# VectorE reads the attention's numerator and denominator in PSUM, tile by tile

## The chip, the cores and the metric

One core of one Trainium2 chip runs the whole program. The metric is device time in microseconds, from launch to end of one execution; the median of several executions counts. TensorE (PE) multiplies matrices into PSUM, VectorE (DVE) and ScalarE (ACT) work on SBUF and PSUM, GpSimd (POOL) works on SBUF and starts the indirect transfers, SyncE (SP) starts the other transfers.

## What is computed

Two blocks follow each other on x, of shape (2, 512, 128), that is 1024 tokens of 128 values. Each block adds a cross-attention to a context of 77 tokens (16 heads of 8 values) and then a mixture of 8 experts, of which each token takes 2. Cut to the part that matters here, one attention is

```python
scores = jnp.einsum('bhqd,bhkd->bhqk', q, k) * SCALE     # block 0 adds a bias
attn = jax.nn.softmax(scores, axis=-1)
attended = jnp.einsum('bhqk,bhkd->bhqd', attn, v)
attended = attended.transpose(0, 2, 1, 3).reshape(B, L_q, D_MODEL)
attended = attended @ Wout.T + b_out                      # block 1: ctx @ W_O + b_O
gate = jax.nn.sigmoid(attended @ Wgate.T + b_gate)        # block 0 only
output = gate * attended + (1.0 - gate) * residual
```

The kernel takes the softmax's division behind the sum over keys: it forms a numerator (probabilities times values) and a denominator (probabilities times ones), both with one column per query and one row per head and value, and divides.

## The kernel before

The 1024 tokens are 8 tiles of 128, two tiles make a query group g (GQ = 256 queries), and there are 4 groups. A unit u is 4 of the 16 heads for one group, so there are 16 units in an attention and units 4g to 4g + 3 belong to group g. Attention a (0 and 1) runs over the units in turns. In turn u, TensorE does the shifted scores of unit u (L1178, in attention 0 with the bias, L1184), the transposed maxima of unit u + 1 (L1162), the scores of unit u + 2 (L1153) and `attend` of unit u - 2 (L1201: 4 matmuls into the numerator bank BNUM, 4 into the denominator bank BDEN, accumulated over the 4 units of the group). From turn 14 on there are no more scores to issue. VectorE reduces the scores of a unit to their maxima (L804), ACT takes the exponential (L654) and copies the maxima into the stack (L638).

The steps that follow on a finished group are laid into the turns by tables (`PE_STEPS`, `DVE_STEPS`, `ACT_STEPS`, `POOL_STEPS`): step `name` of group g comes in turn 4g + 3 + delay on its engine, behind the unit's own work, and in the order of the table where several fall in one turn. Names with a 3 are for the last group. Each engine works in program order; between engines there are only semaphores. The steps named here:

- `attended` (VectorE, L809 to L815): reciprocal of the denominator (L813), times the numerator (L814) into attT. It works on ACT's copy `numden` in SBUF, which ACT makes in `attention` (L643 to L649).
- `attend` (TensorE, L1188) of the first unit of the next group waits on `s_nd`, ACT's copy (L1197), since it overwrites the banks.
- `project` (TensorE, L1205 to L1219): attT times the output weights, in attention 0 also transposed (L1214), into bank BY. In attention 0, ACT then adds the bias to the transposed half (`projected`, L667), VectorE reads the other half (`projected`, L823), TensorE computes the `gate` (L1226, L1227) into the same bank, and ACT takes its tanh (L661). The next group's `project` waits for that tanh.
- `residual` (VectorE, L833 and L835, or L840 and L843) and the statistics, then GpSimd's `deviation` (L500, L501), then `hidden` (VectorE, L796, into hidk), `turn` (TensorE's transposes, L1138), `turned` (ACT, L679), `logits` (TensorE, L1243), `choose` (VectorE, L859 or L862 to L876), `ranks` (TensorE, L1253), `slots` (VectorE, L883 to L889), `send` (GpSimd, L518). The experts begin when all rows are sent.

In turns 3 to 9, GpSimd also subtracts the low halves of the expert weights (L531), 2.4 us each. Behind unit 15, TensorE does some warm-up matmuls between the steps of attention 1 (`WARM_TAIL`), none in attention 0.

## Time and profile before

| | |
|---|---|
| median of 3 runs | 325.83 us (324.19 to 326.91) |
| profiled execution, its span | 324.3 us |
| TensorE busy | 250.7 us (77%) |
| VectorE busy | 155.1 us (48%) |
| ScalarE busy | 118.2 us (36%) |
| GpSimd busy | 137.8 us (42%) |
| chain that ended last | PE 49%, issue 20%, DVE 13%, DMA 6%, POOL 5%, ACT 3% |

The profiled execution's span lies within the times of the runs. The page also cuts the span into 40 slices of 8.1 us, with the busy share of each engine and the granted clock of TensorE in tenths:

```profile
PE   2767999999975539999942989989987338999800
DVE  3878425363775364242211964276878303332205
PEclk9999999999975558999995799999999959999975
```

Attention 0 with its tail lies at about 29 to 120 us, the experts of block 0 behind it, attention 1 with its tail at about 193 to 262 us. TensorE is busy nearly all the time in the loop of units and less so in the tail behind it, where in attention 0 the granted clock is at half for some slices. Busy times of an engine are no critical path: a wait is read from the timeline, by its place.

### The profile page before, as it was taken

To read this page: it belongs to the slowest core of one execution; us is meant where nothing else is said; L and a number is where in the kernel's file an instruction comes from. 1 tells how busy PE (TensorE), PEld (TensorE's weight loads), DVE (VectorE), ACT (ScalarE), POOL (GpSimd) and SP (SyncE) were. 2 spreads that over 40 slices of the span, in tenths; PEclk is the share of its full clock that TensorE was granted. 3 is DMA by queue.
4 is the path that set the end of the run, shared out by engine and by line. 5 is a ranking of instruction groups with operands and counts; after the bars stand their busy time and mean duration, and the time that the engine had idled before them with its cause. 6 is when DMAs were issued, how large, how long until landed. Compare 5 with 4: busy or idle time off the path is not lost.

```text
span 324.3 us, 5466 instructions
## 1 busy us (share of the span) xinstructions
PE 250.7 (77%) x2044; PEld 197.2 (61%) x2044; DVE 155.1 (48%) x497; ACT 118.2 (36%) x206; POOL 137.8 (42%) x178
## 2 busy tenths in 40 slices
PE   2767999999975539999942989989987338999800
PEld 2645766667754427999941775545555328999800
DVE  3878425363775364242211964276878303332205
ACT  4033637755321023443500067965540204423200
POOL 5744602630156441355562400641267631456640
PEclk9999999999975558999995799999999959999975
DMA  7999970200011017000013920200010125001015
GB/s 241 269 224 377 219 161 2 65 3 2 0 36 34 33 33 197 16 20 26 23 36 127 361 116 0 66 1 2 0 37 33 33 82 141 15 31 36 26 29 181
DMA packets 26819, 27.02 MB, mean 83 GB/s; under 512 B 3193, under 2 KB 23844, under 8 KB 26534
## 3 DMA queue, kind: packets, MB, share of 16 engines
q1 hardware_dynamic: 23797, 21.58, 24.6%
q0 software_dynamic: 2560, 4.08, 3.9%
q10 hardware_dynamic: 432, 0.98, 0.9%
q8 instruction: 18, 0.29, 0.4%
q14 instruction: 12, 0.09, 0.1%
HBM read 16.76 MB, written 10.79 MB: 85 GB/s over the span
## 4 chain that ended last, share of the span: by engine, by line
PE 49%; issue 20%; DVE 13%; DMA 6%; POOL 5%; ACT 3%; another core or an unknown queue 1%; SPq 1%; POOLq 0%; DVEq 0%; ACTq 0%
PE ps L1201 8%; PE ps L1406 6%; PE ps L1178 6%; PE ps L1395 5%; PE ps L1162 4%; PE ps L1153 4%; PE ps L1133 3%; PE ps L1184 2%; DMA xres<-x 2%; DMA xe<-back 2%; DVE cst L813 2%; DMA sent<-hidk,slotu 1%; DVE attT L814 1%; PE ps L1217 1%
## 5 line engine op out<-in xcount | busy, mean ns | idle before, releaser
L559 POOL DMA_INDIRECT back<-probT,pairu x48 | 46.5, 970 | 37.4 <-DVE probT L992 15.1
L1133 PE MATMUL ps<-blank,ident 128*128 128x256 f32 x90 | 28.6, 479 | 23.6 <-DMA sent<-hidk,slotu 13.0
L1406 PE MATMUL ps<-w,hT 128*128 128x128 f32 (+1 forms) x384 | 45.0, 274 | 0.0
L804 DVE TENSOR_REDUCE peak<-ps 128x8 f32<-128x616 f32 x32 | 25.5, 798 | 40.2 <-PE ps L1153 40.2
L1406 PEld LDWEIGHTS ps<-w,hT 128*128 128x128 f32 (+1 forms) x384 | 44.2, 183 | 0.0
L654 ACT ACTIVATE probT<-ps 77x1024 f32<-77x1024 f32 x32 | 32.7, 1022 | 27.7 <-PE ps L1184 15.5
L518 POOL DMA_INDIRECT sent<-hidk,slotu x32 | 31.9, 997 | 16.4 <-issue 9.8
L1133 PEld LDWEIGHTS ps<-blank,ident 128*128 128x128 f32 x90 | 21.1, 244 | 28.5 <-issue 14.0
L531 POOL TENSOR_TENSOR w1lo<-hT,w1hi 128x1024 fp32r<-128x1024 f32 x8 | 18.9, 2366 | 40.0 <-ACT w1hi L628 40.0
L1178 PE MATMUL ps<-qst,kst 100*78 100x256 f32 x128 | 29.1, 300 | 1.0 <-ACT qst L638 1.0
L500 POOL TENSOR_SCALAR vare<-mv 128x2 f32<-128x2 f32 (+2 forms) x17 | 3.8, 226 | 52.8 <-DVE mv L786 52.3
L696 ACT ACTIVATE hT<-ps,col 128x384 f32<-128x384 f32 x32 | 17.3, 582 | 24.1 <-PE ps L1395 24.1
L696 ACT ACTIVATE hT<-ps 128x321 f32<-128x321 f32 x32 | 13.3, 441 | 33.2 <-PE ps L1395 33.0
L1395 PE MATMUL ps<-xhi,w1hi 128*128 128x384 f32 (+1 forms) x64 | 22.2, 346 | 1.5 <-DVE xlo L981 1.5
L1178 PEld LDWEIGHTS ps<-qst,kst 100*78 100x78 f32 x128 | 16.9, 148 | 8.4 <-issue 5.8
L1162 PE MATMUL ps<-ident,peak 128*4 128x128 f32 x128 | 19.2, 273 | 2.9 <-DVE peak L804 2.9
L1201 PE MATMUL ps<-probT,vpad 77*32 77x256 f32 x256 | 21.0, 391 | 0.0
L1395 PE MATMUL ps<-xhi,w1lo 128*128 128x384 f32 (+1 forms) x64 | 20.8, 325 | 0.0
L1395 PE MATMUL ps<-xlo,w1hi 128*128 128x384 f32 (+1 forms) x64 | 20.8, 325 | 0.0
L1201 PE MATMUL ps<-probT,onepad 77*32 77x256 f32 x256 | 20.2, 379 | 0.0
L992 DVE TENSOR_TENSOR probT<-ps,row 128x128 f32<-128x128 f32 x24 | 5.5, 285 | 26.6 <-PE ps L1406 23.2
L995 DVE COPY probT<-ps 128x128 f32<-128x128 f32 (+1 forms) x24 | 5.5, 284 | 25.4 <-PE ps L1406 21.9
(158 smaller groups left out, 474.1 us busy)
## 6 DMA issues: line engine op xcount, KB each, us to landing
sent<-blank SPq DMA_DIRECT2D x16, 193.5 KB, 8.5
xe<-sent SPq DMA_DIRECT2D x16, 193.5 KB, 4.0
back<-blank SPq DMA_DIRECT2D x16, 128.0 KB, 4.8
hT<-w1b SPq DMA_DIRECT2D x4, 512.0 KB, 6.0
w<-w2b SPq DMA_DIRECT2D x1, 2048.0 KB, 13.5
xe<-back SPq DMA_DIRECT2D x8, 256.0 KB, 3.5
hT<-w1d SPq DMA_DIRECT2D x4, 512.0 KB, 5.5
w<-w2d SPq DMA_DIRECT2D x1, 2048.0 KB, 11.4
```

The source lines that it names most:

```text
L518: pool.indirect_dma_start(sent[m], bass.IndirectOffsetOnAxis(ap=slotu[:, t, k:k + 1], axis=0), hidk[:, t, k, :], None, bounds_check=NSLOT ...
L531: pool.tensor_tensor(w1lo[:, w, :], raw[:, k % RAWS], w1hi[:, w, :].bitcast(F32), ALU.subtract)\
L559: pool.indirect_dma_start(back[m], bass.IndirectOffsetOnAxis(ap=pairu[0:n, e, c:c + 1], axis=0), ye[0:n, e, c, :], None, bounds_check=NPAI ...
L654: act.activation(probT[0:KV, u % RING].rearrange("p (i q) t -> p i (q t)", i=2), ps[0:KV, BK:BK + 2, :], ACT.Exp).then_inc(s_exp[a], 1)
L696: act.activation(hT[:, e % 2, f, 0:CAP[m]], ps[:, 2 + n % 4, 0:CAP[m]], ACT.Silu, bias=bias).then_inc(s_silu[m], 1)
L804: dve.tensor_reduce(peak[:, u % 2], s, AX.X, ALU.max, negate=True).then_inc(s_peak[a], 1)
L1133: pe.matmul(ps[:, bank, 0:GQ], ident[:], blank[:, 0:2, 0:D], start=True, stop=True)
L1162: last = pe.matmul(ps[ST:ST + Q4, BK + u % 2, i * P:(i + 1) * P], peak[:, u % 2, i, :], ident[:], start=True, stop=True)
L1178: last = pe.matmul(ps[0:KP, BK + q // 2, GQ * (q % 2):GQ * (q % 2) + GQ], kst[0:ST + Q4, b, Q4 * j + q, :], qst[0:ST + Q4, j, at:at + GQ], ...
L1201: last = pe.matmul(ps[32 * q:32 * q + 32, bank, 0:GQ], w, probT[0:KV, u % RING, q, :], start=(j == 0), stop=(j == UG - 1))
L1395: last = pe.matmul(ps[:, 2 + n % 4, 0:EVEN[m]], w[:, e, f * P:(f + 1) * P], x[:, e % 2, 0:EVEN[m]], start=(i == 0), stop=(i == len(parts) ...
L1406: last = pe.matmul(ps[0:n, 6 + e % 2, c * P:(c + 1) * P], hT[:, e % 2, f, c * P:c * P + n], w2[:, e, f, :], start=(f == 0), stop=(f == FC ...
```

## The change

The `numden` copy, its semaphore `s_nd` and ACT's waits are gone. VectorE's `attended` comes one turn earlier (delay 4 in place of 5), waits for TensorE's last `attend` of the group (`s_pv`), and does reciprocal and multiply for one tile of 128 queries after the other, reading both from PSUM; each tile raises `s_att` by one, so a group raises it by GT = 2. `attend` of the next group's first unit and the key stack of attention 1 wait for all tiles by `s_att`. `project` waits for each tile and issues its matmuls per tile.

```diff
-DVE_STEPS = [dict(attended=5, projected3=6, residual3=7, hidden3=9, projected=8, residual=9, hidden=10,
+DVE_STEPS = [dict(attended=4, projected3=6, residual3=7, hidden3=9, projected=8, residual=9, hidden=10,
...
-             dict(attended=5, residual=7, hidden=8, choose=10, slots=11)]
+             dict(attended=4, residual=7, hidden=8, choose=10, slots=11)]
...
-        numden = cst[:, 0:2 * GQ].rearrange("p (i t) -> p i t", i=2)
...
-                g, rest = divmod(u - AHEAD - 1, UG)
-                if rest == UG - 1 and 0 <= g < GROUPS:
-
-                    act.wait_ge(s_pv[a], UG * (g + 1))
-                    if g >= 1:
-                        act.wait_ge(s_att[a], g)
-                    act.copy(numden, ps[:, BNUM:BDEN + 1, 0:GQ]).then_inc(s_nd[a], 1)
...
-                dve.wait_ge(s_nd[a], g + 1)
+                dve.wait_ge(s_pv[a], UG * (g + 1))
                 b, at = divmod(g, GROUPS // B)
-                link(dve.reciprocal(rden, numden[:, 1]))
-                dve.tensor_tensor(attT[:, b, GQ * at:GQ * at + GQ], numden[:, 0], rden, ALU.mult)\
-                   .then_inc(s_att[a], 1)
+                for i in range(GT):
+                    tile = slice(i * P, i * P + P)
+                    link(dve.reciprocal(rden[:, tile], ps[:, BDEN, tile]))
+                    q0 = GQ * at + i * P
+                    dve.tensor_tensor(attT[:, b, q0:q0 + P], ps[:, BNUM, tile], rden[:, tile], ALU.mult)\
+                       .then_inc(s_att[a], 1)
...
-                    pe.wait_ge(s_nd[a], u // UG)
+                    pe.wait_ge(s_att[a], GT * (u // UG))
...
-                pe.wait_ge(s_att[a], g + 1)
...
-                q0 = GQ * at
-                if a == 0:
-                    pe.matmul(ps[:, BY, 0:GQ], weight("out0"), attT[:, b, q0:q0 + GQ], start=True, stop=True)
                 for k in range(GT):
+                    pe.wait_ge(s_att[a], GT * g + k + 1)
+                    tile = attT[:, b, GQ * at + k * P:GQ * at + (k + 1) * P]
+                    if a == 0:
+                        pe.matmul(ps[:, BY, k * P:(k + 1) * P], weight("out0"), tile, start=True, stop=True)
                     o = (GQ if a == 0 else 0) + k * D
-                    last = pe.matmul(ps[:, BY, o:o + D], attT[:, b, q0 + k * P:q0 + (k + 1) * P],
-                                     weight("out0" if a == 0 else "o1"), start=True, stop=True)
+                    last = pe.matmul(ps[:, BY, o:o + D], tile, weight("out0" if a == 0 else "o1"), start=True, stop=True)
                 last.then_inc(s_yz, 1)
...
-                    pe.wait_ge(s_nd[0], GROUPS)
+                    pe.wait_ge(s_att[0], TILES)
```

On VectorE, in the loop of attention 0, the rows around `attended` of group 0 and group 1 stood so in the kernel before (L804 is the maxima reduction of a unit, L823 is `projected` of group 0, cst is the SBUF tensor that held the copy and the reciprocal):

```order
L804 TENSOR_REDUCE peak<-ps 128x8 [waits scores0] x5
L813 RECIPROCAL cst<-cst 128x256 [waits attended_in_sbuf0]
L814 TENSOR_TENSOR attT<-cst 128x256 [waits dve_order]
L804 TENSOR_REDUCE peak<-ps 128x8 [waits scores0] x3
L823 TENSOR_TENSOR hidb<-ps,hidb 128x256 [waits residual_ready,yT_in_sbuf,y_projected]
L804 TENSOR_REDUCE peak<-ps 128x8 [waits scores0]
L813 RECIPROCAL cst<-cst 128x256 [waits attended_in_sbuf0]
L814 TENSOR_TENSOR attT<-cst 128x256 [waits dve_order]
```

and stand so now:

```order
L795 TENSOR_REDUCE peak<-ps 128x8 [waits scores0] x4
L806 RECIPROCAL cst<-ps 128x128 [waits attended0]
L808 TENSOR_TENSOR attT<-ps,cst 128x128 [waits dve_order]
L806 RECIPROCAL cst<-ps 128x128
L808 TENSOR_TENSOR attT<-ps,cst 128x128 [waits dve_order]
L795 TENSOR_REDUCE peak<-ps 128x8 [waits scores0] x4
L806 RECIPROCAL cst<-ps 128x128 [waits attended0]
L808 TENSOR_TENSOR attT<-ps,cst 128x128 [waits dve_order]
L806 RECIPROCAL cst<-ps 128x128
L808 TENSOR_TENSOR attT<-ps,cst 128x128 [waits dve_order]
L817 TENSOR_TENSOR hidb<-ps,hidb 128x256 [waits residual_ready,yT_in_sbuf,y_projected]
```

The step has moved ahead of one reduction, and from group 1 on ahead of `projected` of the group before. On TensorE the same place of attention 0, attend of unit 4, had

```order
L1153 MATMUL ps<-kst,qst 128x312
L1201 MATMUL ps<-probT,vpad 32x256 [waits attended_in_sbuf0,probs0]
L1201 MATMUL ps<-probT,vpad 32x256 x3
L1201 MATMUL ps<-probT,onepad 32x256 x4
L1178 MATMUL ps<-qst,kst 78x256 [waits probs0,maxima_in_stack0]
```

and has now

```order
L1147 MATMUL ps<-kst,qst 128x312
L1195 MATMUL ps<-probT,vpad 32x256 [waits attT_ready0,probs0]
L1195 MATMUL ps<-probT,vpad 32x256 x3
L1195 MATMUL ps<-probT,onepad 32x256 x4
L1172 MATMUL ps<-qst,kst 78x256 [waits probs0,maxima_in_stack0]
```

The matmuls keep their order there, and the first of the attend waits for VectorE's result in place of ACT's copy. On VectorE in the tail of attention 1, `hidden` of group 2 (L796, hidk) stood ahead of `attended` of group 3:

```order
L889 TENSOR_TENSOR slotu<-slot,over 128x4 [waits dve_order]
L796 TENSOR_SCALAR hidk<-xres,mv,rstd 128x128 [waits rstd_ready]
L796 TENSOR_SCALAR hidk<-xres,mv,rstd 128x128
L813 RECIPROCAL cst<-cst 128x256 [waits attended_in_sbuf1]
```

and stands behind it now. The rows now, of group 2 of attention 1 in the loop, show the same order of the two steps (L787 is hidk of group 1):

```order
L795 TENSOR_REDUCE peak<-ps 128x8 [waits scores1]
L806 RECIPROCAL cst<-ps 128x128 [waits attended1]
L808 TENSOR_TENSOR attT<-ps,cst 128x128 [waits dve_order]
L806 RECIPROCAL cst<-ps 128x128
L808 TENSOR_TENSOR attT<-ps,cst 128x128 [waits dve_order]
L787 TENSOR_SCALAR hidk<-xres,mv,rstd 128x128 [waits rstd_ready]
```

In the tail of attention 0, `attended` of group 3 moves likewise from behind `choose` of group 1 to ahead of `projected` of group 2.

## Rows read from the trace of the kernel before

**Rows 1.** Timeline, attention 0, turns 6 and 7: start us, us, engine, line, instruction
```profile
50.97 0.34 PE L1178 MATMUL ps<-qst,kst 100*78 100x256 f32 x1
...
51.11 0.59 ACT L649 COPY cst<-ps 128x512 f32<-128x512 f32 x1 [0.63 <-PE ps L1201]
...
53.17 0.64 PE L1201 MATMUL ps<-probT,vpad 77*32 77x256 f32 x8
...
54.17 0.34 PE L1178 MATMUL ps<-qst,kst 100*78 100x256 f32 x1
...
54.89 2.36 POOL L531 TENSOR_TENSOR w1lo<-hT,w1hi 128x1024 fp32r<-128x1024 f32 x1 [17.22 <-ACT w1hi L628]
...
55.77 1.77 DVE L814 TENSOR_TENSOR attT<-cst 128x256 f32<-128x256 f32 x1
...
57.60 0.70 PE L1214 MATMUL ps<-attT,sqw 128*128 128x256 f32 x2 [0.16 <-DVE attT L814]
```

**Rows 2.** Timeline, attention 1, turns 6 to 7
```profile
209.44 0.70 PE L1178 MATMUL ps<-qst,kst 100*78 100x256 f32 x4
...
211.08 0.64 PE L1201 MATMUL ps<-probT,vpad 77*32 77x256 f32 x8
...
215.78 0.71 PE L1217 MATMUL ps<-sqw,attT 128*128 128x128 f32 x4 [0.99 <-DVE attT L814]
```

**Rows 3.** Single lines of VectorE: duration ns min/median/max, first and last start us
```profile
L813 DVE RECIPROCAL cst<-cst x8: 1739/1743/1753, 54.0 to 243.8; 128x256 f32<-128x256 f32 x8
L814 DVE TENSOR_TENSOR attT<-cst x8: 424/425/2041, 55.8 to 245.5; 128x256 f32<-128x256 f32 x8
L1002 DVE RECIPROCAL wtok<-wden x2: 203/204/204, 121.4 to 257.8; 128x8 f32<-128x8 f32 x2
L992 DVE TENSOR_TENSOR probT<-ps,row x24: 280/282/292, 133.1 to 166.5; 128x128 f32<-128x128 f32 x24
```

**Rows 4.** Timeline at 22.7 us, queries' rotation, VectorE beside GpSimd
```profile
22.71 0.41 DVE L958 TENSOR_TENSOR ropeb<-ps,cst 128x256 f32<-128x256 f32 x1
22.80 0.73 POOL L572 TENSOR_TENSOR qlo<-q,qhi 128x256 fp32r<-128x256 f32 x1 [0.52 <-ACT qhi L720]
```

**Rows 5.** Timelines, turn 14 of attention 0 and of attention 1
```profile
80.50 0.59 ACT L649 COPY cst<-ps 128x512 f32<-128x512 f32 x1 [0.63 <-PE ps L1201]
...
83.40 0.48 PE L1226 MATMUL ps<-row,one 1*128 1x128 f32 x2
...
233.47 0.79 DVE L804 TENSOR_REDUCE peak<-ps 128x8 f32<-128x616 f32 x1
...
236.04 0.44 PE L1138 MATMUL ps<-ident,hidk 128*128 128x128 f32 x2
```

**Rows 6.** Timeline, tail of attention 0
```profile
90.81 0.59 ACT L649 COPY cst<-ps 128x512 f32<-128x512 f32 x1 [0.66 <-PE ps L1201]
...
91.21 0.48 PE L1226 MATMUL ps<-row,one 1*128 1x128 f32 x2
...
92.98 0.38 ACT L661 ACTIVATE norm<-ps 128x256 f32<-128x256 f32 x1 [1.59 <-PE ps L1227]
...
94.99 1.22 PE L1214 MATMUL ps<-attT,sqw 128*128 128x256 f32 x2 [1.79 <-issue]
```

**Rows 7.** Window: us, then busy us of PE, PEld, DVE, ACT, POOL, PEclk, DMA
```profile
94.00:95.00 1.00, 0.01 (x1) 0.01 (x1) 0.96 (x3) 0.00 (x0) 0.38 (x1) 0.52 0.08 29
```

**Rows 8.** Timeline, tail of attention 1
```profile
243.22 0.63 DVE L796 TENSOR_SCALAR hidk<-xres,mv,rstd 128x128 f32<-128x128 f32 x2 [0.43 <-POOL rstd L501]
...
243.91 0.44 PE L1138 MATMUL ps<-ident,hidk 128*128 128x128 f32 x2 [0.27 <-DVE hidk L796]
...
244.81 0.61 PE L1243 MATMUL ps<-router,inT 128*128 128x8 f32 x4 [0.46 <-ACT inT L679]
...
245.89 0.17 DVE L862 COPY logit<-ps 128x16 f32<-128x16 f32 x1
...
247.56 0.42 DVE L840 TENSOR_TENSOR hidb<-ps,row 128x256 f32<-128x256 f32 x1
```

More of the change, by code:

```diff
@@ L337, in two_block_kernel @@
         s_pv = [sem(f"attended{m}") for m in range(2)]
-        s_nd = [sem(f"attended_in_sbuf{m}") for m in range(2)]
         s_att = [sem(f"attT_ready{m}") for m in range(2)]
```

## The prediction

> **What bounds the kernel now.** I read the page first (shares, the 40 slices, the clock), then the timelines of the two attention stages (35 to 120 us and 197 to 262 us), then single lines. Within a unit TensorE runs shifted scores, maxima, scores, attend, one behind the other; the scalar and vector work of the unit lies beside it. In the first attention a unit's attend (53.17 us) starts 2.20 us behind its shifted scores (50.97), and the next unit's shifted scores start 1.00 us behind that [rows 1]; in the second attention the first distance is 1.64 us [rows 2]. So what delays TensorE in a unit delays all that follows. Behind unit 15 the stage is a chain through all engines, and what delays a link there counts too.
>
> The piece that the change touches has two waits. First, attend of unit 4(g+1) overwrites the numerator and denominator banks, so it waits for ACT's copy. The copy starts at 51.11 us, right when the last attend of the group is seen, and takes 0.59 us; TensorE comes to the next attend at 53.17 us [rows 1]. It has 1.4 us to spare. Second, the projection waits for attT. In group 0 of each attention the multiply was stretched, from its median 0.425 us to 1.77 and 2.04 us [rows 1, 3], while GpSimd subtracts weights; TensorE waits 0.16 us for it in the first attention and 0.99 us in the second [rows 1, 2]. The other groups' projections don't wait in the loop.
>
> **The change, part by part.** *VectorE's four instructions.* The reciprocal takes 1.743 us for 256 columns and 0.204 us for 8 [rows 3]. The line through both has 6.2 ns a column, so 128 columns take 0.95 us (bounds: half of the long one, 0.87, and 1.0). A 128x128 two-input operation with one input in PSUM takes 0.282 us [rows 3]. A group is thus 2 x (0.95 + 0.28) = 2.46 us, with bounds 2.3 and 2.6, against 1.743 + 0.425 = 2.17 us. No instruction of this kind reads PSUM in the trace; I take the SBUF reciprocal's time, since 256 columns with an input in PSUM take 0.41 us [rows 4] and with both in SBUF 0.425 us [rows 3]. The Trainium skill's page "VectorE: DVE Perf Modes" (section on the TRN2 errata) has it otherwise: 62 cycles at 0.96 GHz more for an instruction that reads PSUM, 0.065 us. By it a group would be 0.26 us longer, eight times on the path, so the sum would be 2.1 us more. The two rows just named don't agree with it.
>
> *The wait that becomes a long one.* The bank is now free only when both tiles are multiplied, 2.46 us behind the last attend instead of 0.59 us, and 0.06 us pass until TensorE moves (multiply ends at 57.54, TensorE starts at 57.60 [rows 1]). Behind this wait are queued the attend itself and everything else on TensorE; VectorE's next maxima reduction is queued behind the four instructions, and is still in time. The cover is TensorE's work ahead of attend:
> - First attention, group 0: 51.11 + 2.46 + 0.06 = 53.63 against 53.17, +0.46 us. Group 1 has the same order, +0.46.
> - First attention, group 2: no scores are left to issue, so less cover. VectorE can start at 80.50; the attend started 1.00 us ahead of the gate at 83.40, at 82.40 [rows 5]. 83.02 - 82.40 = +0.62.
> - Second attention, group 0: the shifted scores start at 209.44, so the attend before is seen at 209.58 (0.14 later, as 50.97 and 51.11 in rows 1); 212.10 against 211.08 [rows 2], +1.02. Group 1 has the same order, +1.02.
> - Second attention, group 2: VectorE's reduction ends at 234.26; 234.26 + 2.52 = 236.78; the attend started 1.00 us ahead of the transposes at 236.04, at 235.04 [rows 5]. +1.74.
>
> *What it gives back.* The projections of group 0 find attT ready. In the first attention the projection could have started at 54.17 + 2.20 + 1.00 = 57.37 and started at 57.60: -0.23. In the second it could have at 211.08 + 1.00 + 1.64 + 1.00 = 214.72 and did at 215.78: -1.06 [rows 1, 2]. The new multiply reads one input from PSUM, and VectorE's operation of that kind keeps its 0.41 us beside a GpSimd subtraction [rows 4], so I don't let GpSimd hold it. In the Trainium skill, "SBUF — State Buffer", section "Who interferes with whom", such an instruction doesn't compete with GpSimd; the trace agrees.
>
> *At nothing:* ACT's copy (8 x 0.59 us; ACT is waiting for the next shifted scores there, and has more room without it; cover gone, nothing waits), and the transposed projection in two halves, the same columns in all.
>
> *Tail of the first attention.* By the order, VectorE now takes attended(3) before projected(2) and choose(1). It starts at 90.81 and ends at 93.27; projected(2), 0.41 us, ends at 93.68. It frees what the gate of group 2 waits for, which ran at 91.21 [rows 6]: +2.5. From the gate's start to the tanh are 1.77 us (91.21 to 92.98), the tanh and the step to TensorE take 0.45. Then comes project(3), which needs that bank: 93.74 + 1.77 + 0.45 = 95.96 against 94.99, +0.97. But TensorE stands still for 2.4 us before that gate. In the kernel before, TensorE had paused for 1.79 us ahead of 94.99 us [rows 6], and the granted clock fell there, 0.52 on the mean of 94 to 95 us [rows 7], which is the 1.2 GHz level; the pair of projection matmuls takes 1.22 us there against 0.70 us at 2.4 GHz [rows 1, 6]. At the low clock the gate's 1.77 us become 1.77 x 1.22 / 0.70 = 3.1, +1.3. I take that: the pause is longer and earlier than the one that lowered the clock before. Tail: +2.3.
>
> *Tail of the second attention.* attended(3) now stands ahead of hidden(2). VectorE is free at 242.79 (hidk at 243.22 less its wait of 0.43), ends the four at 245.25, hidden(2) (0.63) at 245.88; the transposes that ran at 243.91, 0.27 us behind their wait for it, run at 245.94: +2.0. Some of this is returned: choose(2) started at 245.89 though the logits had ended at 245.42, since attended(3) held VectorE. New: 245.94 + 1.98 - 0.47 = 247.45; the residual of group 3 started 1.67 us behind choose(2), so at 249.1 against 247.56 [rows 8]: +1.5. All to the end hangs on it: sends, expert rows.
>
> **Sum.** First attention: 0.46 - 0.23 + 0.46 + 0.62 + 2.3 = +3.6. Second: 1.02 - 1.06 + 1.02 + 1.74 + 1.5 = +4.2. Together +7.8 us; against the profiled execution 324.3 + 7.8 = 332.1. The median is 325.83, 1.5 above the profiled one; the change adds to it, 333.6. My times lean to the long side (0.08 us of overlap between unlinked VectorE instructions is left out), so I say 333.2.
>
> **Rivals.**
> - *The clock falls in the second tail too.* TensorE would stand still for about 2.3 us before the transposes of group 2, where warm-ups kept it at full clock. For: a pause of that kind lowered the clock in the first attention [rows 7]. Against: warm-ups lie around it. Transposes, logits, warm-ups and projection of the last groups would run at half: some 1.3 us up to the last residual, 1 us behind it. 335.5.
> - *GpSimd still holds the multiply* in group 0 of the second attention, where VectorE's new place (209.6 to 212.1) lies on a weight subtraction. One multiply would wait about 1.9 us more: 335.1. Against: rows 4.
> - *A dearer start from PSUM.* An instruction's fixed part is 0.15 us by rows (0.204 less 8 columns at 6.2 ns); if reading PSUM added half of it, four times a group and in eight groups, that were 2.4 us: 335.6. Against it are the 0.41 us of rows 4. The page's figure, above, would give 335.3.
> - *Not slower.* The reciprocal might run from PSUM at one column per 1 ns, as the multiply does. Then a group is 4 x 0.28 = 1.1 us. It decides at 2.0 us a group in the first attention and 1.4 in the second: below, no attend waits. Left are -0.23, -1.06, and in the tails about -0.5 and 0: 325.8 - 1.8 = 324.0. Against it speaks that 248 columns more cost 1.54 us [rows 3], which is the divide and not the read. The same outcome, by another road, is a wait that is hidden in some slack that I don't see.
> - Inside the forecast: the clock stays at 2.4 GHz through the second gate, 1.3 us less, 331.9.
>
> **How the numbers follow.** Forecast 62%, second tail's clock 18%, GpSimd's hold 6%, PSUM dearer 6%, not slower 8%. The range of the forecast alone is 331 to 334.5; the rivals above reach 335.6, and two at once 338. Below I go to 329, where the group takes 2.3 us (eight times 0.16 less) and the clock stays up. 329 to 338 leaves out the not-slower case and some double mishaps. About 1% is what a measurement of this kernel can tell from no change; 1% is 3.3 us, so the forecast is past it. Not slower gives 2% faster and 6% same; 4% more of same are the forecast's low edge. Slower 88%.
>
> **What would show each step.** Right: reciprocals of 0.95 us and multiplies of 0.28 us; TensorE's first attend matmul of units 4, 8, 12 waiting for VectorE's multiply by 0.5, 0.5, 0.6 us in the first and 1.0, 1.0, 1.7 us in the second attention; no wait ahead of the group-0 projections; the gate of group 2 waiting 2.4 us for hidb; the transposes of group 2 in the second tail waiting 2 us for hidk. Wrong: a reciprocal near 0.3 us, a multiply near 2 us beside GpSimd, or a first gate matmul of group 2 at full clock and early.

## The result, and the profile after

| | before | after |
|---|---|---|
| median | 326.37 us (324.19 to 329.22) | 353.16 us (350.28 to 362.63) |
| profiled execution, its span | 324.3 us | 349.2 us |
| TensorE busy | 250.7 us | 271.9 us |
| mean granted clock of the span | 0.898 | 0.836 |

The ratio is 1.080, with a 95% interval of 1.069 to 1.091: slower, by over three times what I had forecast. Every ratio with an interval here is taken over the runs that lie within 1.5% of the fastest of their kernel; medians and ranges are of all runs. The changed kernel also scatters over 12 us where the kernel before scatters over 5. Its page has, in 40 slices of 8.7 us:

```profile
PE   3777999999956739999924989889898809999900
...
PEclk9969999999965555999985899996855865999985
```

The slices at 5 behind the first attention are wider than before, and there are new low ones near 240 us and from 253 us on, in the loop of the second attention, where TensorE's clock had been full throughout.

What the change itself does came out as forecast. VectorE's single lines in the changed kernel (duration in ns, min/median/max; L806 is the reciprocal, L808 the multiply):

```profile
L806 DVE RECIPROCAL cst<-ps x16: 945/948/959, 54.0 to 265.4; 128x128 f32<-128x128 f32 x16
L808 DVE TENSOR_TENSOR attT<-ps,cst x16: 290/291/292, 55.0 to 266.4; 128x128 f32<-128x128 f32 x16
```

A group is 2 x (0.948 + 0.291) = 2.48 us. The timeline shows TensorE's attend waiting for it six times; here the first and last of the first attention, and the three of the second, with the multiply of one beside GpSimd's subtraction (which started at 221.25 and took 2.36 us). Line numbers are those of the kernel that a row comes from; in the changed kernel L1195 is attend:

```profile
56.67 0.64 PE L1195 MATMUL ps<-probT,vpad 77*32 77x256 f32 x8 [0.48 <-DVE attT L808]
86.98 0.64 PE L1195 MATMUL ps<-probT,vpad 77*32 77x256 f32 x8 [0.51 <-DVE attT L808]
221.25 2.36 POOL L529 TENSOR_TENSOR w1lo<-hT,w1hi 128x1024 fp32r<-128x1024 f32 x1 [0.27 <-ACT w1hi L626]
222.92 0.29 DVE L808 TENSOR_TENSOR attT<-ps,cst 128x128 f32<-128x128 f32 x1
223.35 0.64 PE L1195 MATMUL ps<-probT,vpad 77*32 77x256 f32 x8 [1.05 <-DVE attT L808]
235.51 0.64 PE L1195 MATMUL ps<-probT,vpad 77*32 77x256 f32 x8 [1.04 <-DVE attT L808]
252.11 1.08 PE L1195 MATMUL ps<-probT,vpad 77*32 77x256 f32 x8 [1.56 <-DVE attT L808]
```

The last row holds what I had missed: 1.08 us for matmuls that take 0.64 in the others. Windows of the changed kernel (us, then busy us of PE, PEld, DVE, ACT, POOL, then PEclk, DMA):

```profile
234.00:236.00 2.00, 0.96 (x14) 0.61 (x18) 1.97 (x6) 0.88 (x2) 0.04 (x1) 1.00 0.00 0
236.00:238.00 2.00, 1.54 (x19) 0.89 (x12) 0.58 (x1) 0.37 (x1) 0.64 (x1) 1.00 0.00 0
238.00:240.00 2.00, 2.00 (x11) 1.16 (x9) 0.00 (x0) 1.31 (x2) 0.00 (x0) 0.58 0.00 0
...
250.00:252.00 2.00, 0.55 (x5) 0.21 (x4) 1.93 (x5) 1.39 (x2) 1.70 (x2) 1.00 0.10 33
252.00:254.00 2.00, 1.89 (x17) 0.71 (x17) 0.48 (x2) 0.00 (x0) 1.39 (x3) 0.50 0.22 70
```

TensorE is busy for 0.96 and for 0.55 us of 2 in the windows with these two waits, and the granted clock is at its lower level (1.2 GHz) from 238.3 us and from 252.0 us. It did not fall behind the first wait, at 223.35 us.

By stages of the two profiled executions, read from the first and last rows of each in the timelines (us; the stage of units runs from the first scores to the last attend, the tail to the last `slots`; the last column is the kernel e2_fill below):

| stage | before | after | difference | e2_fill |
|---|---|---|---|---|
| start to first scores | 26.63 | 30.46 | +3.8 | 26.39 |
| units, attention 0 | 64.12 | 64.86 | +0.7 | 71.30 |
| tail | 22.76 | 23.20 | +0.4 | 24.40 |
| to the first up matmul | 12.04 | 14.73 | +2.7 | 13.12 |
| experts, block 0 | 40.57 | 43.30 | +2.7 | 42.09 |
| to the first scores | 24.36 | 25.08 | +0.7 | 24.46 |
| units, attention 1 | 52.11 | 62.53 | +10.4 | 54.62 |
| tail | 15.10 | 16.96 | +1.9 | 16.67 |
| all to the end | 66.7 | 68.1 | +1.4 | 70.3 |

The start-up's 3.8 us don't come from the change: the clock was low from 16.5 to 23.3 us, ahead of every changed instruction. The same kernel profiled again (e13_after_again) had 26.35 us there, and the kernel before with another change (e8_weights_early) 30.02.

### The profile page after: what moved, and what is told of

It reads as the page before. It is cut to its first block, busy times and chain, and to the rows that moved or that the text cites. A ratio compares the mean times of both kernels' runs of the same rounds, so it can differ in the third digit from the quotient of the medians.

```text
span 349.2 us, 5484 instructions
## 1 busy us (share of the span) xinstructions
PE 271.9 (78%) x2052; PEld 210.4 (60%) x2052; DVE 153.7 (44%) x513; ACT 114.2 (33%) x198; POOL 137.7 (39%) x178
## 4 chain that ended last, share of the span: by engine, by line
PE 62%; DVE 14%; DMA 8%; issue 7%; POOL 5%; ACT 3%; POOLq 1%; SPq 0%; DVEq 0%; ACTq 0%
PE ps L1399 11%; PE ps L1388 10%; PE ps L1195 10%; PE ps L1172 5%; PE ps L1127 4%; DVE cst L806 4%; PE ps L1156 4%; PE ps L1147 3%; PE ps L1178 2%; POOL sent L516 2%; DMA xres<-x 2%; PE ps L1211 2%; DMA sent<-hidk,slotu 2%; POOL back L557 2%; PE ps L1375 2%
## 5 line engine op out<-in xcount | busy, mean ns | idle before, releaser
L1127 PE MATMUL ps<-blank,ident 128*128 128x256 f32 x90 | 31.2, 512 | 24.5 <-DMA sent<-hidk,slotu 13.2
L1127 PEld LDWEIGHTS ps<-blank,ident 128*128 128x128 f32 x90 | 22.8, 264 | 30.2 <-issue 14.6
L516 POOL DMA_INDIRECT sent<-hidk,slotu x32 | 33.0, 1032 | 14.4 <-issue 10.1
L1195 PE MATMUL ps<-probT,vpad 77*32 77x256 f32 x256 | 22.7, 428 | 5.1 <-DVE attT L808 5.1
L1388 PE MATMUL ps<-xhi,w1hi 128*128 128x384 f32 (+1 forms) x64 | 24.1, 377 | 1.3 <-DVE xlo L975 1.3
L1388 PE MATMUL ps<-xlo,w1hi 128*128 128x384 f32 (+1 forms) x64 | 22.5, 351 | 0.0
L1388 PE MATMUL ps<-xhi,w1lo 128*128 128x384 f32 (+1 forms) x64 | 22.4, 349 | 0.0
L1195 PE MATMUL ps<-probT,onepad 77*32 77x256 f32 x256 | 22.2, 419 | 0.0
L973 DVE CAST xhi<-ps 128x384 fp32r<-128x384 f32 (+1 forms) x16 | 8.3, 516 | 22.8 <-PE ps L1375 22.8
L1147 PE MATMUL ps<-kst,qst 96*128 96x312 f32 x64 | 17.8, 361 | 0.0
```

Of the source, the lines that this page charges most:

```text
L516: pool.indirect_dma_start(sent[m], bass.IndirectOffsetOnAxis(ap=slotu[:, t, k:k + 1], axis=0), hidk[:, t, k, :], None, bounds_check=NSLOT ...
L1127: pe.matmul(ps[:, bank, 0:GQ], ident[:], blank[:, 0:2, 0:D], start=True, stop=True)
L1147: last = pe.matmul(ps[:, BS + i, 0:Q4 * KP], qst[0:ST, j, at + i * P:at + (i + 1) * P], kst[0:ST, b, Q4 * j:Q4 * j + Q4, :].rearrange("p q ...
L1195: last = pe.matmul(ps[32 * q:32 * q + 32, bank, 0:GQ], w, probT[0:KV, u % RING, q, :], start=(j == 0), stop=(j == UG - 1))
L1388: last = pe.matmul(ps[:, 2 + n % 4, 0:EVEN[m]], w[:, e, f * P:(f + 1) * P], x[:, e % 2, 0:EVEN[m]], start=(i == 0), stop=(i == len(parts) ...
```

## The experiments

The theory after the first look: TensorE's pauses, of about 1 us, cost more in clock than in waiting (called the pauses theory below). The rivals: reading PSUM or the tiling does it; the new place of the step on VectorE; a fixed effect of the program in some other place.

### e1_late_attend: the same waits, one turn later

```
-                    if AHEAD <= u < UNITS + AHEAD:
-                        attend(a, u - AHEAD)
+                    v = u - AHEAD
+                    if 0 <= v < UNITS and (v % UG or v == 0):
+                        if v % UG == 1 and v > 1:
+                            attend(a, v - 1)
+                        attend(a, v)
```

> The changed kernel, with one edit: the first attend of a new group (units 4, 8, 12) is issued one turn later, right ahead of the attend of the next unit. All work and all reads of PSUM stay; VectorE gets a whole turn for its four instructions. Pauses theory (TensorE's waits for VectorE cost 5 us by themselves, and the low clock that they set off costs the rest): no attend waits for attT, TensorE instead waits some 0.5 us for the exponential in the shortened turn; the clock in the units of attention 1 stays at the high level; 326 to 336 us. Rival (reading PSUM on VectorE or the projection by tiles is what costs): no gain, 348 us or more. Rival (the low clock is chance and not tied to the waits): attention 1's units stay at about 62 us with half clock in them, 345 us or more.

363.09 us (355.67 to 365.63) against 333.51 for the kernel before on that chip: 1.096 (1.081 to 1.111). My expectation of 326 to 336 us missed. The wait for the multiply was gone, and others stood in its place in the second attention (us in all, times, longest):

```profile
PE ps L1132 <- DVE hidk L787: 3.4, 2, 2.0
PE ps L1156 <- DVE peak L795: 1.5, 3, 0.8
```

The clock still fell, at 240.1 us. Taking away one wait says nothing while VectorE's step comes as early and TensorE pauses all the same. The total also fits the rival that reading PSUM or the projection by tiles costs (348 us or more); e3, e4 and e6 decide that one.

### e2_fill: the waits stay, TensorE works through them

```
+                    if a == 1:
+                        if u // UG >= 2:
+                            pe.wait_ge(s_yread, GROUPS + u // UG - 1)
+                        warm_up(3 if u // UG == 3 else 2, BY)
```

> The changed kernel, with dummy matmuls (two of 256 columns at groups 1 and 2, three at group 3) put in front of the waiting attend in attention 1 only, into the bank of the projection, which is free there. VectorE's work and TensorE's waiting point stay; only the pause is filled. Pauses theory: the direct waits stay (1.0, 1.0 and 1.6 us less the filling), but the clock holds its high level through attention 1's units, which fall from 62.5 us to about 55; total 342 to 346 us. If the clock is chance, or falls for another reason than the pauses: 350 to 353 us, as the changed kernel.

344.16 us (340.94 to 350.37), 1.030 (1.016 to 1.044) of the same runs of before. Its timeline at the place of the wait, and the windows over the units of attention 1 in the kernel before, the changed one and this one:

```profile
222.72 0.59 PE L1127 MATMUL ps<-blank,ident 128*128 128x256 f32 x2
223.41 0.64 PE L1199 MATMUL ps<-probT,vpad 77*32 77x256 f32 x8
```

```profile
190.50:242.60 52.10, 48.36 (x471) 28.32 (x469) 33.04 (x80) 33.08 (x49) 17.19 (x16) 1.00 0.06 17
```

```profile
201.60:264.20 62.60, 56.80 (x471) 31.76 (x469) 31.71 (x87) 31.40 (x46) 17.94 (x17) 0.85 0.04 14
```

```profile
201.80:256.40 54.60, 51.86 (x484) 30.56 (x483) 31.37 (x86) 31.40 (x46) 17.18 (x16) 1.00 0.05 17
```

The mean clock of the stage is back at 1.00, and the stage takes 54.62 us: 2.5 more than before, which are the waits less what the change gives back. The matmuls that were added compute nothing that is used; the stage is 7.9 us shorter with them. This is the direct test of the theory for the second attention; e7 and e14, below, repeat it. It doesn't separate two readings: that the pause is gone, or that there are more dense matmuls in the loop at all. No run puts the same matmuls elsewhere in it.

### e3_copy_then_wait, e4_whole_group, e6_move_only: which part of the change

e3 is the kernel before with ACT's copy and VectorE on SBUF, only the step moved and attend waiting for its result:

```
-DVE_STEPS = [dict(attended=5, ...
+DVE_STEPS = [dict(attended=4, ...
-                    pe.wait_ge(s_nd[a], u // UG)
+                    pe.wait_ge(s_att[a], u // UG)
```

> The kernel before (ACT's copy, VectorE on SBUF, whole groups), with VectorE's step one turn earlier as in the change and TensorE's attend waiting for attT in place of the copy. Nothing on VectorE reads PSUM here. Pauses theory: the chain is copy 0.59 + reciprocal 1.74 + multiply 0.42 us, so the attends wait some 0.9 us in attention 0 and 1.4 to 2.1 us in attention 1, longer than in the changed kernel; 350 to 365 us. Rival (PSUM reads or the projection by tiles cost): at most 335 us.

373.27 us (364.36 to 377.75) against 333.51 for before. The median is past the expected range and the fastest run at its upper end. The longest wait of attend is 1.86 us here, in attention 1, with the copy in the chain. The step that moved reads no PSUM here (the reductions of the scores do, as in every version), and all four runs are far above the 335 us of the rival, so reading PSUM isn't needed for the loss.

e4 is the changed kernel with one reciprocal and one multiply of 256 columns from PSUM.

> The changed kernel, with one reciprocal and one multiply over both tiles (256 columns) in place of two each, still from PSUM, attT raised for both at once. VectorE's chain is 2.17 us in place of 2.44. Pauses theory: each of six attends waits 0.27 us less; 1.6 to 2.2 us directly, and no more than that unless the clock keeps up: 346 to 351 us; if the shorter pauses of about 0.8 us no longer lower the clock in attention 1, 340 us. Rival (work by tiles is what costs): below 335 us.

351.11 us (347.48 to 352.89), 1.054 (1.041 to 1.066). This is at the top of the expected range and far above the rival's 335 us: work by tiles is not what costs either. (The ratios of e1, e2 and e4 stand against 333.51 us, on another chip, and are not to be set beside the 1.080.) In attention 1 the clock fell at 237.3 us, behind waits of 0.86 us. In attention 0 it fell at 70.1 us, where the last wait of attend ahead of it had been 0.30 us:

```profile
67.57 0.64 PE L1192 MATMUL ps<-probT,vpad 77*32 77x256 f32 x8 [0.30 <-DVE attT L805]
```

So in that execution no pause near 1 us stood ahead of the fall in attention 0. The rows of e4 answer the question of what a read from PSUM costs:

```profile
L804 DVE RECIPROCAL cst<-ps 128x256 f32<-128x256 f32 x8 | 14.1, 1757 | 5.0 <-PE ps L1192 5.0
L805 DVE TENSOR_TENSOR attT<-ps,cst 128x256 f32<-128x256 f32 x8 | 3.4, 425 | 0.8
```

1757 and 425 ns against 1743 and 425 with both inputs in SBUF [rows 3].

e6 is the kernel before with only the first two of e3's lines, so attend waits for the copy alone.

> The kernel before with nothing but the delay of attended at 4 in place of 5; ACT still copies numerator and denominator, and attend waits for the copy alone. If the pauses of TensorE ahead of attend are the cause, this kernel has none and stays at the time of before, within 1% or up to 4 us above it for the order in the tails, and the clock stays full in the units of attention 1. If the new place of the step on VectorE (ahead of a reduction, against a copy that ends later) does the damage, it comes near the 373 us of the kernel that copied and then waited.

354.92 us (352.44 to 368.54), 1.069 (1.059 to 1.078), where the kernel before has 331.62 on that chip. This missed, and taught most: the delay alone, with no PSUM read, no tiles and ACT's copy in place, costs 7%. TensorE waits for something else (timeline, with the DVE rows ahead of the first wait):

```profile
221.07 1.75 DVE L813 RECIPROCAL cst<-cst 128x256 f32<-128x256 f32 x1 [1.30 <-ACT cst L649]
222.86 0.42 DVE L814 TENSOR_TENSOR attT<-cst 128x256 f32<-128x256 f32 x1
223.20 0.79 DVE L804 TENSOR_REDUCE peak<-ps 128x8 f32<-128x616 f32 x1
...
224.05 0.60 PE L1162 MATMUL ps<-ident,peak 128*4 128x128 f32 x4 [0.86 <-DVE peak L804]
...
235.36 0.44 PE L1138 MATMUL ps<-ident,hidk 128*128 128x128 f32 x2 [0.83 <-DVE hidk L796]
```

The maxima reduction, and later hidk, are queued behind the early step, TensorE pauses for them, and at 236.0 us the clock falls (window of this kernel):

```profile
236.00:238.00 2.00, 1.74 (x8) 1.62 (x8) 0.01 (x1) 0.20 (x1) 0.06 (x1) 0.51 0.04 8
```

So it isn't the wait on s_att as such. VectorE's step, 2.17 us long and one turn early, stops TensorE for 0.83 to 0.86 us here by whichever wait is nearest. In the changed kernel the wait at attend came first, and no wait of over 0.4 us for a reduction or for hidk stands in the units of attention 1 beyond the first turn.

### e5_last_group_late: the order in the tails

`attended3=5` is added to both tables of the changed kernel.

> The changed kernel, except that VectorE's attended of group 3 comes at its old delay of 5, in both attentions, so behind projected and choose (attention 0) and behind hidden of group 2 (attention 1). If the tail terms of the prediction (+2.3 and +1.5 us) are real costs of the order on VectorE, this kernel gets about 3 to 4 us back from the changed one, 347 to 350, with the tails at the lengths of before (22.8 and 15.1 us). The rival: the tails' lengths are set by the sends and by the low clock and not by this order (the changed kernel's first tail was only 0.4 us longer than before's); then the time is that of the changed kernel, 350 to 354, and the tails are 23.2 and 17 us.

359.41 us (346.89 to 360.88). The total says nothing: in the profiled execution the clock fell at 223.7 us, right behind the first wait, and the units of attention 1 took 74.3 us. The stage does: from the last attend of attention 0 to the landing of the last send are 29.95 us in the kernel before, 31.36 in the changed one, 29.81 here. The order costs 1.5 us there, where I had 2.3. The second tail did not come back to the 15.1 us that I expected: with the old order it takes 16.55 us, hardly less than the 16.67 to 16.88 us of e2, e7 and e14 with the new one. TensorE waits 0.6 us for hidk there, in place of 2.1 in e2 and e14, but the clock was low in the first 6.7 us of that tail, so order and clock are not separated.

### e7_fill_both and e14_fill_shift: filling in both attentions

e7 is e2 with one dummy matmul ahead of the attend of units 4 and 8 of attention 0. e14 fills unit 12 too, and has the five tiny matmuls of e11, below, so that e11 is e14 without the filling.

> The kernel with dummy matmuls ahead of the waiting attend in attention 1, with one dummy matmul more ahead of the attend of units 4 and 8 of attention 0. The pauses theory expects the units of attention 0 at 65.5 to 67 us with full clock (they were 71.3 with a stretch at half clock at 70.8 to 81.1 us in the kernel with filling in attention 1 alone, and 64.9 in the changed one, which had no such stretch), and those of attention 1 at 54.6 again; total 338 to 343. The rival, that the stretch at half clock in attention 0 has another cause than these waits, expects it in about the same place, 70 to 80 us, and a total of 342 to 346.

> The changed kernel with dummy matmuls ahead of every waiting attend of both attentions (one in attention 0, two or three in attention 1) and the five tiny ones in start-up. Both causes of the excess over the prediction should be gone, and what is left is what I had predicted: waits of 2.5 us in attention 1, 1.6 us in attention 0, the tails. So 334 to 338 where the kernel before has 331.6, ratio 1.01 to 1.025. If the filling in attention 0 only moves the fall of the clock on (as it did to 86 us with units 4 and 8 filled), the ratio is 1.025 to 1.035, the units of attention 0 take 68 us or more.

e7: 342.32 us (338.9 to 345.98), 1.032 (1.024 to 1.040). e14: 338.2 us (334.06 to 338.88), 1.035 (1.027 to 1.043). In both the units of attention 1 keep the full clock (54.7 and 54.2 us; the window of e14):

```profile
199.80:254.00 54.20, 51.88 (x485) 30.64 (x483) 31.41 (x86) 31.37 (x46) 17.18 (x16) 1.00 0.05 16
```

In attention 0 of e7 the low stretch moved from 70.8 to 86.2 us, behind the wait ahead of unit 12, which was left unfilled (that attend starts at 83.6), so 70.3 us where 65.5 to 67 were expected; e14 has none, and takes 64.7. That says little for attention 0, since the changed kernel, e5 and e17 have no low stretch there either, without filling. For the whole time the filling is clear: e14's four runs (up to 338.88 us) lie below all four of e11, 357.55 to 366.91 us on the same chip, which differs by the filling alone. The 1.01 to 1.025 that I expected of e14 missed: its ratio is 1.035 though the clock kept up in the units of both attentions. Part of what is left over sits in the next point.

### e13_after_again, e11_code_shift, e16_copy_kept, e17_code_phase: repetition, and the late rows

> The changed kernel once more, as it is. The theory under test says that the same instructions can lose the clock at other places: the pauses are the same 0.5 and 1.0 us, and whether the clock falls at one is left open by them. It expects the units of attention 1 again to have a stretch at half clock (as in all six kernels that pause there without filling), the units of attention 0 to have one or not (the kernel with filling in attention 1 alone runs the same instructions there, and had one at 70.8 us, with 71.3 us for the stage against 64.9), and a start-up of 26.5 us in place of 30.5. Against the kernel before in the same runs: ratio 1.06 to 1.09. If instead the place is fixed by the program, the stretches are where they were, with attention 0 free of one.

356.24 us (345.94 to 366.38; before in these runs 326.75, so 1.09 by the medians). The same program: the start-up took 26.35 us, the units of attention 0 75.4 (64.9 the first time), those of attention 1 73.8 (62.5). Behind the same wait that kept the clock in the first execution (223.35 us there), it fell this time, at 230.4 us (timeline, windows):

```profile
228.67 0.64 PE L1195 MATMUL ps<-probT,vpad 77*32 77x256 f32 x8 [1.05 <-DVE attT L808]
```

```profile
230.00:232.00 2.00, 2.00 (x14) 0.98 (x14) 0.00 (x0) 1.38 (x2) 1.56 (x1) 0.61 0.00 0
```

Where the clock falls is thus a matter of the execution; that it falls somewhere in attention 1's units is not. It did in all ten profiled executions with the early step and no filling there (the changed kernel twice, e1, e3 to e6, e11, e16, e17), and in none of the three with filling (e2, e7, e14). Of the three profiled executions without the early step, those of the kernel before and of e9 have no fall in the units of attention 1. In e8 it fell at 241.2, behind a wait of 1.1 us for inT that the kernel before has as well, without a fall:

```profile
237.53 0.61 PE L1243 MATMUL ps<-router,inT 128*128 128x8 f32 x4 [1.05 <-ACT inT L679]
```

So a pause of 1 us doesn't always cost the clock, and the kernel before isn't safe from it either; it has one profiled execution here.

The last open point was the 5.4 us between the end of the tail and the end of the experts of block 0. About 1.0 of it are the last sends, which land 8.2 us behind the last `slots` in place of 7.2, part of the tail's cost in e5. Then the expert rows land late: between the start of the warm-up and the first matmul on the rows are 4.05 to 4.54 us in the ten profiled executions of the changed kernel and those made from it except e17, and 2.69 to 2.70 in the other six. In each of the ten a packet of 16 KB of the instruction queue lies between the two, in none of the six. The timeline, and the DMA view of the changed kernel from 126.5 to 132 us (queue, kind: packets, MB, share), which has the packet of 16 KB; in the kernel before no such row stands between the same points:

```profile
126.68 2.90 PE L1127 MATMUL ps<-blank,ident 128*128 128x256 f32 x6 [4.55 <-DMA sent<-hidk,slotu]
131.03 1.58 PE L1375 MATMUL ps<-ident,xe 128*128 128x128 f32 x6 [1.45 <-DMA xe<-sent]
```

```profile
q8 instruction: 1, 0.02, 1.2%
```

e11 adds five matmuls of 8 columns to the changed kernel's start-up, e16 puts a copy on ACT back (256 zeros in SBUF), e17 writes the 13 warm-up matmuls of the start-up as 67 of 50 columns:

```
-            warm_up(WARM_START)
+            for _ in range(67):
+                pe.matmul(ps[:, BR, 0:50], ident[:], blank[:, 0:2, 0:25], start=True, stop=True)
```

> The changed kernel with five tiny dummy matmuls (8 columns) in TensorE's start-up, which move every later 16 KB fetch of TensorE's code some 20 instructions ahead in the program. In the five kernels without ACT's copy one such fetch (128.6 us in the changed kernel) lies between the last send and the first expert rows of block 0, the rows land 4.2 us behind the start of the warm-up in place of 2.7 us, and the clock comes back 6 us into the experts. If the fetch or its place does this, the rows now land 2.7 us behind the warm-up's start, the experts of block 0 take 40.6 us in place of 43, and the time is 3 to 4.5 us less than that of the changed kernel. If the late rows have another cause (the missing copy itself), both stay as they are: 4.2 us, 43 us, and the time of the changed kernel within 1 us.

> The changed kernel with a copy on ACT put back at its old place and waited for by attend beside the multiply; it copies 256 zeros within SBUF and nothing reads them, so it stands for ACT's lost instructions alone. If the late expert rows of block 0 come from ACT's shorter program, the rows land 2.7 us behind the start of the warm-up (as in the kernels with the copy) and the experts of block 0 take 40.6 us, so 4 to 5 us less than the changed kernel by the stages. If they come from TensorE's projection by tiles or the doubled VectorE steps, the rows still land 4.2 us or more behind it and the experts take 43 us. The waits of attend (0.5 and 1.0 us) and the low clock in attention 1 stay in both cases, with a total of 346 to 362.

> The changed kernel with the 13 warm-up matmuls of the start-up written as 67 of 50 columns each, about the same columns in all, which moves TensorE's later code by some 216 instructions. If the 16 KB fetch between the last send and the first rows of block 0 belongs to TensorE's code, it moves by most of a fetch's 256 instructions, to some 3 us behind the first up matmul as in the kernel before, and if it is what makes the rows late, they land 2.7 us behind the warm-up's start and the experts take 40.6 us. If the fetch stays between the two, it is another engine's; if it moves and the rows stay late, it is not the cause.

e11: 366.55 us (357.55 to 366.91), rows 4.5 us behind the warm-up's start, the packet still there. e16: 353.22 us (351.56 to 355.58), 1.083 (1.074 to 1.091), rows at 4.4 us. So a shift by 20 instructions doesn't bring the rows back, and ACT's missing copy isn't the cause. e17: 371.94 us (369.24 to 374.86), 1.137 (1.127 to 1.146), since its start-up of small matmuls takes 22 us more than e13's. But behind that, the packet is gone from the place (code packets at 124.5 and at 153.6 us) and the rows are early, in time for the end of the warm-up:

```profile
145.08 2.90 PE L1127 MATMUL ps<-blank,ident 128*128 128x256 f32 x6 [4.53 <-DMA sent<-hidk,slotu]
147.77 0.85 PE L1375 MATMUL ps<-ident,xe 128*128 128x128 f32 x3
```

2.69 us, as in the kernel before, in place of 4.35. Only TensorE's code was changed, and the packet moved. The late landing goes with where that packet falls; how the packet would delay the rows isn't shown. Why a shift by 20 left it in place isn't settled. In the Trainium skill, "Advanced Engine Details and Errata", section "ISA Cache", a line of an engine's code is 16 KB, 256 instructions; the packets here have 16 KB, and the 256 of e17's expectation is that page's figure, which no run shows alone. The experts of block 0 took 42.38 us in e17, not the 40.6 expected: the clock came back 4 us into them (6 in the changed kernel, just ahead of them in the kernel before). So of the 5.4 us, 1.0 are the sends, some 1.65 the rows, and 2.7 the clock's late return. What decides the return stays open. It isn't the change alone: in e8, made from the kernel before and with its rows in time, the clock came back 4.7 us into the experts and they took 42.69 us.

### e8_weights_early and e9_weights_early_warm: tries on the kernel before

```
-WEIGHT_TURNS = [[6, 7, 8, 9], [3, 4, 5, 6]]
+WEIGHT_TURNS = [[4, 5, 7, 8], [2, 3, 4, 5]]
```

> The kernel before with GpSimd's weight subtractions in turns 4, 5, 7, 8 of attention 0 and 2 to 5 of attention 1 in place of 6 to 9 and 3 to 6, so that none lies beside VectorE's multiply of group 0. It tests the term -0.23 - 1.06 us that the change was to give back: if the prediction is right in it, the multiplies take 0.42 us in all eight groups, TensorE doesn't wait ahead of the projections of group 0, and the time is 1 to 1.5 us less than that of before, hardly more than can be measured. The rival: the subtraction then holds another VectorE instruction (a reduction), and nothing is won or up to 1 us lost.

331.1 us (326.52 to 337.77), 0.995 (0.990 to 1.001). The multiplies take 0.483 us at most in place of 2.04, and from the shifted scores of unit 7 to those of unit 8 of the second attention are 3.10 us in place of 4.16: the 1.06 us of my term exactly. In the total it can't be told from nothing.

e9 adds `WARM_TAIL = [3, 2]` in place of `[0, 2]`.

> A try at a kernel that beats both: the one before with GpSimd's weight subtractions a turn or two earlier and three warm-up matmuls a turn in the tail of attention 0, where it had none. By the theory that TensorE's pauses lower the clock, the stretch at half clock in that tail (94 to 125 us) gets shorter or goes, and the tail with the way to the experts is 1 to 4 us shorter: ratio 0.985 to 1.0. The rival: the warm-ups stand in the way of the chain's own matmuls (at half clock three of them are 1.4 us a turn), the ratio is 1.0 to 1.02.

326.69 us (324.94 to 328.79), 1.003 (0.999 to 1.007). The tail got less than the 1 to 4 us expected. Windows of the tail of attention 0, in the kernel before and in this one:

```profile
94.00:104.00 10.00, 6.46 (x20) 4.84 (x20) 6.17 (x30) 1.64 (x4) 5.84 (x9) 0.50 0.10 34
```

```profile
94.00:104.00 10.00, 9.38 (x64) 7.62 (x63) 6.80 (x33) 1.91 (x5) 6.24 (x9) 1.00 0.10 34
```

The clock stays up for 24 us more, and the tail with the way to the experts is only 0.6 us shorter (34.19 against 34.80). e8, without the warm-ups and with the clock low from 97.8 us, has 34.25, so the warm-ups and the clock that they keep give 0.06 us between them. Two things can cancel there. The warm-ups stand in the chain's way, as the rival said: the gate of group 2 starts 1.87 us behind the last attend in place of 0.47 in e8 and in the kernel before. And the higher clock shortens what follows: from the gate of group 3 to its tanh are 1.77 us in place of 2.97. This pair of kernels doesn't separate the two. No version here beats the kernel before beyond what can be measured.

## Why the prediction was right or wrong, point by point

- *VectorE's group*: 2.46 us forecast, 2.48 measured. The reciprocal runs from PSUM as from SBUF, 0.014 us apart for 256 columns (e4), and the multiply wasn't held beside GpSimd (0.292 us at most). The rivals of a dearer start and of GpSimd's hold are out. By the table of the Trainium skill's "VectorE: DVE Perf Modes" (section on the TRN2 errata) an instruction that reads PSUM has 62 cycles more, an estimate of 0.065 us. No row here shows that: e4 has 0.014 us for the reciprocal and nothing for the multiply.
- *The waits at attend*: 0.46, 0.46, 0.62 and 1.02, 1.02, 1.74 forecast; 0.48, 0.48, 0.51 and 1.05, 1.04, 1.56 measured. The units of attention 1, with the clock kept up, are 2.0 to 2.6 us longer in e2, e7 and e14, where the terms with the give-back make 2.7; those of attention 0, at full clock in the changed kernel, are 0.7 us longer, where the terms make 1.3. As waits they were right.
- *The give-back*: 1.06 us measured as such in e8, and no wait ahead of the projections of group 0 in the changed kernel. Right.
- *First tail*: the gate of group 2 waited 2.48 us for hidb and ran at half clock, as said:

```profile
98.33 0.72 PE L1219 MATMUL ps<-row,one 1*128 1x128 f32 x2 [2.48 <-DVE hidb L817]
...
101.26 0.38 ACT L652 ACTIVATE norm<-ps 128x256 f32<-128x256 f32 x1 [6.53 <-PE ps L1220]
...
101.70 0.79 PE L1209 MATMUL ps<-attT,sqw 128*128 128x128 f32 x2 [0.31 <-ACT norm L652]
```

From the gate to the tanh are 2.93 us, where I had 3.1, and the projection of group 3 starts 6.38 us behind the end of the last attend in place of 4.25: 2.1 later, where I had 2.3. But the stage up to the last send is only 1.5 us longer by e5. I had passed the whole delay of that projection on to the end of the stage; some 0.6 us of it are taken up behind it, and where isn't measured.

- *Second tail*: +1.5 forecast, +1.9 measured in the changed kernel, +1.6 to 1.8 in e2, e7 and e14. TensorE's transposes waited 2.1 us for hidk in e2 and e14, as forecast. But e5, with the old order, is 1.5 us over before as well, so that the number came out doesn't show that the order made it. The rival of the clock, at 18%, came true in part: the clock was low for some stretch of this tail in every profiled execution with the early step, where it had fallen in the loop ahead or fell in the tail itself.
- *The step that failed*: the six waits were put into the sum at their own length, and the clock behind them at nothing. I had the pause of 1.79 us and the fall of the clock behind it [rows 6, 7], asked of the two tails whether new pauses would do the same, and never asked it of the loop, though I had just worked out pauses of 1.02 to 1.74 us there. The prediction has no word on why the loop would be safe. Its windows stood at full clock in the kernel before, in spite of two pauses of that size (0.99 us at 215.78 [rows 2] and 1.05 us at 237.53); that shows that the clock can survive such pauses, not that more of them are free. What the runs showed in place of the step: the clock fell in all ten profiled executions with the early step and no filling in attention 1, and in none of the three with filling. This is worth 7.9 us in one execution and 19 in another in attention 1 alone, and in some 10 more in attention 0, where the link to the waits is not shown.
- *Not in the sum at all*: the expert rows (1.65 us) and the clock's late return in block 0 (1.8 to 2.7 us). No row of the kernel before pointed to them. With them and the clock of the loop, the sum has an account: of the 24.9 us between the two profiled executions, 6.6 are in the terms that I had added up to 7.8 (waits, give-back, tails, sends), 7.9 are the clock in attention 1, 4.4 the rows and the clock in block 0, 3.8 the start-up, and 2.2 lie in the stages just ahead of the second attention and behind its tail. e14, where no unit ran at half clock, is 11.5 us over before by the medians.

## What to carry to other kernels

A pause of TensorE in a loop that otherwise keeps it busy is priced at its length only as long as the clock holds; ask of every new wait, in the loop first, what the matmuls behind it cost at half clock. Moving a long VectorE step ahead of a short one that TensorE needs made such a pause here, whatever TensorE then waited on. If the wait must stay, dummy matmuls in it are cheap to try. A wide spread of the runs (12 us here, against 5 before) is a hint to look where the clock falls.

## What the runs showed that I had not expected

- Pauses of 1.05 and 1.04 us were followed by a fall of the granted clock to 1.2 GHz 1.7 and 2.8 us behind their ends (228.67 in e13, 235.51 in the changed kernel); the same pause at 223.35 us was not.
- The same program takes 62.5 or 73.8 us for the same 16 units, by where the clock falls.
- 134 matmul passes of 50 columns took 28.75 us (0.21 us each) at the start of e17, where 26 of 256 columns take 7.1 to 8.5 us (0.27 to 0.33 each) in the other kernels.
- A code packet of 16 KB between a send and a gather went with rows that land 1.4 to 1.8 us later, in ten of ten profiled executions.
- Dense matmuls in the pauses took the whole program from 366.55 to 338.2 us (e11 and e14, which differ by them alone).
